# Another order of the steps on every engine, and other PSUM banks, in a four-layer graph network kernel

## The reference

```python
# layer 0: e[i,k] = u1[idx1] + u2[idx2], leaky 0.1, masked, softmax over rows
out = einsum('bik,bkl->bil', softmax(where(adj > 0, e, NEG), axis=1), h) + x @ self_weight
# layer 1: attention over A, layernorm, then a GIN with a two-step MLP
h_gat = relu(layernorm(einsum('bmn,bnh->bmh', softmax(scores) * A, h)))
h_gin = (1 + eps) * h_gat + einsum('mn,bnh->bmh', A, h_gat)
out = relu(relu(layernorm(h_gin @ W1 + b1)) @ W2 + b2 + h_gat)
# layer 2: attention with leaky 0.2, then elu
out = elu(einsum('bij,bjo->bio', softmax(where(adj > 0, e, NEG)), Wh) + bias)
# layer 3: one weighted matrix a3 = softmax(where(adj > 0, e3[rank of the edge], NEG)), its diagonal apart
out = einsum('ij,bjg->big', A * M, h0) + einsum('ij,bjg->big', A * (1 - M), h1) + bias
```

## Time and profile before

| what | value |
|---|---|
| median of 3 runs | 1053.7 us (1052.65 to 1054.69) |
| time of the profiled execution | 1053.7 us |
| its span, first to last instruction | 1052.0 us |
| outside the span | 1.7 us |
| mean granted TensorE clock | 0.959 |
| busy, us | PE 964.9, DVE 873.9, ACT 629.9, POOL 554.2 |
| moved to and from HBM | 10.43 MB read, 8.39 MB written |

### The profile page before, as it was taken

The page is one execution under the profiler, slowest core; times in us unless marked ns, Lnnn a source line. Parts: engine busy times, 40 slices in busy tenths (PEclk is TensorE's granted clock), DMA queues, the critical chain, the costliest instruction groups (busy, mean ns, idle before and its releaser), DMA issues. The chain is left out here.

```text
span 1052.0 us, 21202 instructions
## 1 busy us (share of the span) xinstructions
PE 964.9 (92%) x7355; PEld 913.3 (87%) x7355; DVE 873.9 (83%) x2532; ACT 629.9 (60%) x1641; POOL 554.2 (53%) x1169
## 2 busy tenths in 40 slices
PE   4788999998999999999989899999899999997996
PEld 4678998988999889998988899898899999886996
DVE  5978797899868888897989878689998888778873
ACT  2444556676677664667574764676537775677631
POOL 3425344574558662665565554547436655465840
PEclk8778899999999899999999999999999999999999
DMA  6020000000011010002000101100100100000004
GB/s 137 2 59 2 2 2 1 2 1 2 1 41 41 2 41 2 2 9 73 2 1 1 41 1 41 41 1 2 41 2 2 40 2 2 1 2 1 1 1 121
DMA packets 38490, 20.17 MB, mean 19 GB/s; under 512 B 3184, under 2 KB 37872, under 8 KB 38384
## 3 DMA queue, kind: packets, MB, share of 16 engines
q1 hardware_dynamic: 36512, 18.42, 6.6%
q10 hardware_dynamic: 1872, 0.40, 0.2%
HBM read 10.43 MB, written 8.39 MB: 18 GB/s over the span
## 5 line engine op out<-in xcount | busy, mean ns | idle before, releaser
L639 PE MATMUL ps<-HE,PT 128*128 128x129 f32 x2048 | 240.5, 277 | 5.9 <-issue 4.8
L639 PEld LDWEIGHTS ps<-HE,PT 128*128 128x128 f32 x2048 | 234.7, 193 | 9.3 <-issue 7.9
L925 ACT ACTIVATE Y<-X,SM 128x128 f32<-128x128 f32 x512 | 203.9, 490 | 44.8 <-POOL SM L1083 44.8
L1291 DVE SCALAR_TENSOR_TENSOR PT<-ps,CE,maskT 128x512 f32<-128x512 f32 x256 | 174.1, 742 | 12.2 <-PE ps L763 5.4
L1068 POOL TENSOR_TENSOR SM<-ST 128x8 f32<-128x8 f32 x96 | 32.0, 333 | 276.6 <-DVE ST L1154 276.5
L1079 POOL TENSOR_TENSOR SM<-SM,minus_half 128x8 f32<-128x8 f32 x96 | 162.2, 1690 | 7.6
L639 PE MATMUL ps<-W,HT 128*128 128x128 f32 (+1 forms) x768 | 126.5, 312 | 1.7 <-ACT HT L918 1.6
L639 PEld LDWEIGHTS ps<-W,HT 128*128 128x128 f32 x768 | 116.1, 194 | 11.2 <-ACT HT L918 2.0
L1154 DVE BATCH_NORM_STATS2 ST<-X 128x6 f32<-128x128 f32 x512 | 104.9, 278 | 16.8 <-DMA X<-in_x_dram 13.7
L656 PE MATMUL ps<-ident,Y 128*128 128x128 f32 x640 | 86.2, 280 | 10.1 <-ACT Y L925 8.0
L656 PEld LDWEIGHTS ps<-ident,Y 128*128 128x128 f32 x640 | 74.0, 145 | 14.2 <-ACT Y L925 12.8
(11 more groups left out here) (262 smaller groups left out, 2356.6 us busy)
## 6 DMA issues: line engine op xcount, KB each, us to landing
X<-in_x_dram SPq DMA_DIRECT2D x32, 256.0 KB, 3.5
out_dram<-X SPq DMA_DIRECT2D x32, 256.0 KB, 2.8
adj_raw<-in_adj_dram SPq DMA_DIRECT2D x4, 256.0 KB, 3.7
W<-in_L_gnn_W_dram SPq DMA_DIRECT2D x1, 128.0 KB, 5.7
...
```

The costliest lines, as they stand in the source:

```text
L639: return nc.tensor.matmul(o, w, m, start=start, stop=stop, skip_group_check=True)
L925: a = A(dst[:, n, 0:F], src[:, n, 0:F], func, scale=SM[s][:, S_RSTD, n:n + 1], bias=SM[s][:, S_SHIFT, n:n + 1])
L1291: a = V.scalar_tensor_tensor(out=PT[r][:, j, :], in0=o, scalar=CE[s][:, c:c + 1], in1=maskT[:, j, :].bitcast(F32), op0=ALU.max, op1=ALU.mult)
```

## The change

TURNS and HOMES get other values. The step functions, the instructions within a step, the waits' code and all tiles stay as they are. Because HOMES changes with the order, 779 of 901 PSUM tiles get another bank. The strings, cut to their first lines where they are long:

```diff
--- before.py
+++ after.py
@@ -118,35 +118,35 @@
     ("eturn", 4, "pe act dve"),
 ]
 TURNS = {
-    "pe": ("ggggg0110102010g212001231424300130411003344100115152255330125202312323230203413134505010000110104114"
-           "1541424525455405025231012122234262422637667643746226377334323346434346768487866446886757578773837785"
-           "8583488488545955959959656a9a9a56a6a7979969669969766a575665a7777878777ab66b8a8ba67aa7bb8aa8bb978b89b8"
...
-    "act": ("gg01102g102g0133244001120031140055110035141021230231203302211303502101001324141055441202550442530214"
-           "1521542332264247632376446227533243467336444838668763678455773635788574684847588957955598a696a66a5897"
-           "9766995a679967655976977778ab86a6b78867ab7a88ba7aa9abb8889bcabca9d8da9bca88bd989cba9a99baaaedecccecab"
...
+    "pe": ("ggggg10012010120g12002114234300330101431004415051151225330520232132130223323101344055000140011100514"
+           "1142445120454505525201312123224624222676736674346226373743324443664633734864864876688573787578377785"
+           "858348848849595559956595a6a9956a6aa9796979966695696675675aa7777877877b6ab6ba8ba8aa67b7aa8bb88798b9b8"
...
+    "act": ("gg01102g012g0214343002131005411500110310542012303221010332211330520314004102151150442023104554252045"
+           "14123125635222443672746346223237443336464476688386673785375476538785748487456889795855596aa9666a9895"
+           "676997566969757a5967797778b8a6b6a7868baa7778b8aaab89ab898cba9baddc89a8bcbad8899b9caa99abaaeedcc9cecd"
...
-    "dve": ("g021gggg1010g0g2004311210001112425300431103304101421502352021313355242023132320043113544552005001010"
-           "1140402114455125154330225014612425372224262627666334746662737372334834346673848776364588846477578887"
-           "4637855838894784565799a5998965a999a5566a5a59979966a866795a76695aa77b667787777b6a88ab6aabbb79abbb8aa7"
...
-    "pool": ("01201031420153240132453012015430510021421562734626237463748873386584475989a5969a6576a597ab6786787bba"
-           "bc89dac898dbace9dcaed9ebc9ebdafbcffaefdcdfcedfbefdbcefcdeffe"),
-    "sp": ("354100617228394a5b6c7d8e9fedcbaf"),
+    "dve": ("g201gggg0101g02g004312110001115223304004113034120515412302203331551220323123423001341544525050301001"
+           "2014104014145125154503224501645122357224226267266633474662736372443686734734386677383446888778578876"
+           "344875853889478476955a985599965999a5a66a5a959896769669656a7795aaab7766778777b67aba88aa6b97bbbabb7a8c"
...
+    "pool": ("0121004312015342013253014203514501002142156237462623476837478338658474598a95969a655769a7ab67867b78ba"
+           "bcd98a88cd9bace9caded9ecb9ebdfbacfafefdcbdfcedfcefefcdbdeffe"),
+    "sp": ("034502611728394a5b67cd8e9fceadbf"),
 }
-HOMES = ("0123456701235647012356470351264703570357012364570123016423016420517351357642601357416012760140217634"
-         "5021756341745613745610261026103745246107361520473604752316047523041675252673041452145214567302121245"
...
+HOMES = ("0123456701234567012345670123456127021702134705621347627163471247053060601247677601247534536047530647"
+         "5123064753064753064127517230645146514672350142631745026371450263714502605052637014054012563470127256"
...
```

More of the change, by code:

```diff
@@ L120 @@
 TURNS = {
-    "pe": ("ggggg0110102010g212001231424300130411003344100115152255330125202312323230203413134505010000110104114"
-           "1541424525455405025231012122234262422637667643746226377334323346434346768487866446886757578773837785"
-           "8583488488545955959959656a9a9a56a6a7979969669969766a575665a7777878777ab66b8a8ba67aa7bb8aa8bb978b89b8"
-           "ba8cba8bc89dccbdad9cb8a89dd9989caa9aaca9a9e9aacecdcdeccbecedbdcdeeb9dbddde9e9bebbbceecefbfefbffabbcd"
-           "fcfadafffdffdfcfccceccdeddccfdfdeeddffdeebefefffeebfeecdfcffbdcedfefef"),
@@ new lines @@
+    "pe": ("ggggg10012010120g12002114234300330101431004415051151225330520232132130223323101344055000140011100514"
+           "1142445120454505525201312123224624222676736674346226373743324443664633734864864876688573787578377785"
+           "858348848849595559956595a6a9956a6aa9796979966695696675675aa7777877877b6ab6ba8ba8aa67b7aa8bb88798b9b8"
+           "8bab8a8cd9bdcb9dcab8cc8da9d9989ac9aaaca9a9e9eacacdcdecbceecdcdb9deddedbdb9eee9beebbcbebefcbfbfbffcda"
+           "cffadaffdffdffcfccceccedccdfddfededdffdeeeefeeffecbfeffcffdbdcebdfefef"),
@@ new lines @@
+    "act": ("gg01102g012g0214343002131005411500110310542012303221010332211330520314004102151150442023104554252045"
+           "14123125635222443672746346223237443336464476688386673785375476538785748487456889795855596aa9666a9895"
+           "676997566969757a5967797778b8a6b6a7868baa7778b8aaab89ab898cba9baddc89a8bcbad8899b9caa99abaaeedcc9cecd"
+           "cbdec9b9ddbcbacde9ebdeebdcbbefbfcfdcebacfdaeadfefddffcfccfccedefdfecfdfdedffbeedfeefefccffecbddbfede"
+           "ffef"),
+    "dve": ("g201gggg0101g02g004312110001115223304004113034120515412302203331551220323123423001341544525050301001"
+           "2014104014145125154503224501645122357224226267266633474662736372443686734734386677383446888778578876"
+           "344875853889478476955a985599965999a5a66a5a959896769669656a7795aaab7766778777b67aba88aa6b97bbbabb7a8c"
+           "8da9bb88ba8888cdbc99dbcc8aad9bc89dcaea9c9c9aadaba9cecdddecc99eecdedbeddeecbb9ceead9eebfbdabcfbfbbdef"
+           "ffccfffadebabffffddeccfccefcfdcccdfdeeddffdedeefeefdeffeceffbfdcfebfedf"),
@@ new lines @@
+    "pool": ("0121004312015342013253014203514501002142156237462623476837478338658474598a95969a655769a7ab67867b78ba"
+           "bcd98a88cd9bace9caded9ecb9ebdfbacfafefdcbdfcedfcefefcdbdeffe"),
+    "sp": ("034502611728394a5b67cd8e9fceadbf"),
+}
+HOMES = ("0123456701234567012345670123456127021702134705621347627163471247053060601247677601247534536047530647"
+         "5123064753064753064127517230645146514672350142631745026371450263714502605052637014054012563470127256"
+         "0314725725762576203145765476520314765312047653210471074653210563271405632714052146305302174617641530"
+         "2020204716523025024371675024135035671246076074607435127516043272742351607423751462051463746374632057"
+         "1463205714632057105476324756375106324510637251406351472067203514267627603514063527061435270614352706"
+         "1436152704365217064523170645235121271064264710264713571026435710715071507126434234650721653465021734"
+         "0560732107456327104563104565656562371054654372160547051632635126470764076435012412076413520352037645"
+         "2103764106524124065637124506371271237124506124560412563712054637210546372104562137231045671024356576"
+         "1024357602143576057650765210473604521734650645021763746374750427156304271425630714256304721472147562"
+         "1")
```

11 lines of the change are left out of this document (removed).

## The result

The changed kernel takes 1083.2 us (median of 4 runs, 1082.9 to 1086.1) against 1054.2 us: ratio 1.0279, interval 1.0252 to 1.0306. That is 29 us slower; 2.6 us slower was forecast, with a range that ended at 1062. The profiled execution has a span of 1083.3 us, 31.3 more than the old 1052.0.

A forecast was written before the change was run, and what follows sets the result against it. PE, busy 964.9 of 1052.0 us, was taken as the bound, the DMA queue at the end. Stall terms of 6.4 us, cut to 4.4, less 1.8 for stores gave +2.6 on 1053.7: 1056.3 us; 8-in-10 range 1048.5 to 1062.

The forecast's parts named there:

- The stores, -1.8 us: End of the kernel: c's stores leave earlier under matmuls, ten DMAs instead of twelve remain for the end; -1.8 us.
- The start, +0.5 us: Start to 1.self0: 0.agg0 at 81 us, +4.1, mostly given back as 2.feat0 fills 1.agg0's wait; +0.5 us.
- The rival that put the start's gain first: 0.agg0 not late, before about 79 us, so the hole before 1.agg0 is filled: -3.9 us; 1048.3 us; chance 0.28.
- 157 to 200, +1.0: 157 to 200 us: 0.gin1's bank wait closes, three other waits open; PE 1.0 us late at 196 us, bounds -3 and +3.
- 200 to 260, +2.5: 200 to 260 us: ACT and POOL steps drawn ahead delay 0.spread2a to about 235 us; +2.5 us, bounds 0 and +5.
- 320 to 357, +2.4: 320 to 357 us: ACT's 2.top2 behind 6.scale0, PE waits for 4.gin1; +2.4 us, bounds 0 and +5.9.
- The rest, 0 between -5 and +5: 410 to 975 us: closing and opening waits of one to four us each, booked at 0, between -5 and +5 us.
- I keep three quarters: Whole kernel: later waits partly absorb a late PE, so 6.4 us of stall terms count as 4.4.
- Clearly slower: the waits also take the clock: Rival: full stall terms, four more from 410 us on, about 1 us of clock each; 1066 us, at half 1060; chance 0.12.

The follow-up runs named there:

- stores_only: Kernel before with only the new order of the last six stores (c, e, a, d, b, f); ratio 0.9992 to the kernel before.
- new_788_end: Kernel before, with the new order from PE entry 353 to the end, stores too, banks behind it renamed; ratio 1.0143 to the kernel before.
- s4_775_897: Kernel before, with new order and banks from PE entry 353 to 403 only; ratio 1.0202 to the kernel before.
- s5_tail: Kernel before, with new order and banks from PE entry 404 to the end, stores too; ratio 1.0079 to the kernel before.
- unpaired4: Changed kernel with four DVE moves: 6.gat1, 9.gat1, d.gat1 and d.elu2 each put behind later steps; ratio 1.0267 to the kernel before.
- undo_788_end: Changed kernel, with the old order from PE entry 353 to the end, old stores, banks behind it renamed; ratio 1.0149 to the kernel before.
- undo_775_end: Changed kernel, with old order and banks from PE entry 353 to the end, old stores too; ratio 1.0212 to the kernel before.
- undo_775_897: Changed kernel, with old order and banks from PE entry 353 to 403 only; ratio 1.0306 to the kernel before.
- unpaired: Changed kernel with eight DVE moves putting gat1 or elu2 behind steps that read PSUM, away from POOL's statistics; ratio 1.0331 to the kernel before.
- norm_later: Changed kernel with five PE moves: transposes that wait for a scaled tile go behind the step that follows them; ratio 1.0365 to the kernel before.
- tail_fix: Changed kernel with several DVE moves and one ACT move (e.gatl1 behind d.mlpb1) after 788 us; ratio 1.0296 to the kernel before.
- pool_200_260: Changed kernel with POOL's 3.gats1 behind 4.stat1 again and ACT's 3.gat1 behind 4.scale1; ratio 1.0363 to the kernel before.

## Why the prediction was wrong

**The stores, -1.8 us: right.** c's DMAs left ahead of the others, SP's timeline of the changed kernel has the twelve from 1047.05 on over 32.86 us, and the end after PE's last matmul is 6.4 instead of 8.3 us, -1.9. It is too small for the timing of stores_only, and is read from traces.

**The start, +0.5 us: +0.9, its steps right, its size within the scatter** (at entry 27 four kernels with the new start are between -3.6 and +0.9, and new_788_end, s4_775_897 and s5_tail, with the old one, at -1.2, -1.6 and -3.4). 0.agg0 came at 82.6, 5.8 us late (4.1 were worked out), 2.feat0 filled the hole, 1.agg0 waited 0.94 instead of 3.88 us. The rival that put the start's gain first is out: where 0.agg0 did come before 79 us (78.0 in unpaired4's trace), PE was 3.6 us early at entry 27 and 11.4 us late at entry 150 all the same.

**104 to 157 us: no term at all, +4.9 us.** I went from the start straight to 157 us. PE has waits of 0.4 to 1.4 us from 0.spread1a to 0.att1a there, and a granted clock of 0.50 from 126.6 to 133.2 us, where the old kernel has 1.00 from 116 to 157.

**157 to 200, +1.0: measured +2.5** (entry 54 to 73). The bank wait of 0.gin1 did close. What I did not see: 3.self0 waits 2.52 us for POOL's LOWB, which stands behind a 1.gats1 that begins 7.9 us later than before (155.3 us) and takes 8.1 us (7.5 before) beside DVE's 0.gat1, and 3.norm1 waits 2.16 us.

**200 to 260, +2.5: +1.3, its place right.** 0.spread2a was put at 235 us plus what was late before. 9.9 us were late at entry 85, and it began at 244.97. The old 2.51 us wait is filled.

**320 to 357, +2.4: +2.6, with luck.** From 256 to 358 us the changed kernel's trace loses 2.6 us, at another wait (1.8 us at 1.agg3); the forecast wait at 4.gin1 is 0.4 us. In undo_788_end, whose lists are the same up to there, 4.gin1 waits 1.9 us for ACT and the stretch costs 5.6 us; so it is in undo_775_end, undo_775_897 and unpaired4 (5.6 each).

**The rest, 0 between -5 and +5: this is the step that failed.** "I see no side on which they fall. I book them at 0." Lateness went from 12.4 us at entry 172 (398.7 us) to 29.6 at entry 441 (967.1 us), +17.2, and the last 70 us added 3.6. Up to 780 us the 0 held in this trace (+12.4, then +12.6); it failed behind. new_788_end shows that 20 us belong to the order behind 788 us alone, its last 70 us among them, for which the prediction had no term. Of the waits that I named, 7.mlpc1, c.norm0 and b.norm1 (1.6, 1.8 and 1.2 us before) did close and 6.norm2 opened (1.1 us); those that made the loss, e.norm1 (2.0 us), f.norm0 (2.6), d.mlpb1 (2.8), d.spread2a (3.0) and f.norm2 (5.2, was 2.3), I had not named. I had read which waits close and which open, against the old times of the producers; but a closed wait is bounded by its old size, 34.3 us over 565 us, about half of it in pieces under 1 us, while an opened one has no bound. From 775 to 885 us hardly anything was there to close (2.9 us in 110), so there the side was to be seen. It was less plain from 885 to 1044 us, where 11.0 us were there to close and the larger part of the loss lies (+12.3).

**"I keep three quarters": wrong as well.** undo_775_end was 21.8 to 22.5 us late over its last 250 us, undo_788_end 18.4 to 20.1. Nothing is given back there, where PE is busy for 93 to 97% of the time. The sum has a slip too: three quarters of 6.4 us are 4.8, not 4.4, so the forecast should have read 1056.7 us.

**The clock was left to a rival.** PE's busy time grew 12.7 us with 18.6 us of new time without work, 0.7 us for each. The changed kernel's waits of 2.2 to 3.0 us at 3.norm1, 4.norm1, f.norm0, d.mlpb1 and d.spread2a end at 184.1, 243.1, 873.3, 925.3 and 975.1 us, and the granted clock is 0.50 or 0.51 from 184.5, 242.6, 874.0, 925.2 and 976.4 us on. "Clearly slower: the waits also take the clock" had the mechanism, with about 1 us for each stall term, and 1060 to 1066 as its time; it had chance 0.12 and was too small because it used the same stall terms. The Trainium skill (TensorE: Matmul & The Clock Gate, HAM oscillation) tells of a kernel in which an array left waiting is throttled again and starts its next matmuls cold; the trace agrees, with a granted clock of 0.95 where it was 0.99.

**What stays open.** Held POOL steps explain between nothing and some 8 of the 31 us: 3.3 and 4.6 to 8.3 us in two traces, nothing in the timings. The rest after 788 us are single waits of 1.3 to 5.2 us for DVE, ACT and POOL steps that stand a place or two too late in their lists, and each repair tried (unpaired, norm_later, tail_fix, pool_200_260) moved the wait to another step. Banks were not tried alone. A single exchange that carries the loss was not found. I suppose that there is none, and that four lists and a bank map fit each other or they don't; that isn't shown.
